# First node products from a turned x inside the sort and bucket stages; six basis pieces and the edge factors inside node stage two

## The reference

```
# every layer: x = layernorm(x + layer(x))
# layer 0: relu(concat(x[src], x[dst]) @ W0.T + b0) summed at src    # = relu(P[src] + Q[dst]), P = x @ W0a.T + b0, Q = x @ W0b.T
# layer 1: h = x @ W1.T, 8 heads; score * (1 + et_emb[type8]) * weight, softmax over dst; sum of h[src]; + x; layernorm
# layer 2: x @ Wself.T + mean of neighbours @ Wneigh.T + bias; layernorm
# layer 3, twice: w[r] = sum over 30 bases of att[r, b] * basis[b]; gated messages by type of 2; + x @ root + bias
```

## Time and profile before

| | |
|---|---|
| runs, us | 1919.64, 1920.72, 1919.0 |
| the profiled execution, us | 1921.72 |
| its span, us | 1919.7 |
| TensorE busy | 1587.8 us, 83% |
| VectorE busy | 1174.5 us, 61% |
| GpSimd busy | 720.3 us, 38% |
| ScalarE busy | 472.1 us, 25% |
| DMA | 249.14 MB, mean 130 GB/s |

### The profile page before, as it was taken

One profiled execution on the slowest core, in us unless ns is written; L12 is line 12 of the kernel. 1 busy time (PEld: TensorE's weight loads), 2 busy tenths in 40 slices (PEclk: granted clock), 3 DMA queues, 4 the chain that ended last, 5 costly groups with the idle time before them and its releaser, 6 DMA issues. The chain is left out here.

```text
span 1919.7 us, 26410 instructions
## 1 busy us (share of the span) xinstructions
PE 1587.8 (83%) x7213; PEld 962.6 (50%) x7214; DVE 1174.5 (61%) x2310; ACT 472.1 (25%) x884; POOL 720.3 (38%) x605
## 2 busy tenths in 40 slices
PE   6854886786498999998777369997598899999998
PEld 5750653335444555554544335554246545864486
DVE  5768889993375777775577876664865732122222
ACT  3301113433112555554344210000110111001100
POOL 0008777865094776660000447775330010000000
PEclk9996898998698999999898679999799999999999
DMA  0007764006703766682387337776105202430033
GB/s 25 0 18 263 257 210 121 2 2 214 269 27 104 208 197 187 186 169 43 132 348 303 118 109 211 210 210 152 28 1 157 84 1 92 150 110 1 0 137 136
DMA packets 76357, 249.14 MB, mean 130 GB/s; under 512 B 14901, under 2 KB 28582, under 8 KB 68346
## 3 DMA queue, kind: packets, MB, share of 16 engines
q1 hardware_dynamic: 38618, 147.08, 21.3%
q0 software_dynamic: 34592, 96.87, 19.0%
q10 hardware_dynamic: 3072, 4.20, 0.8%
HBM read 215.93 MB, written 32.00 MB: 129 GB/s over the span
## 5 line engine op out<-in xcount | busy, mean ns | idle before, releaser
L669 POOL DMA_INDIRECT tab_slots<-slot_words,slot_address x160 | 253.1, 1582 | 224.8 <-issue 215.0
L698 POOL DMA_INDIRECT e_rows<-tab_h,idx_h x176 | 178.6, 1015 | 286.3 <-POOLq L50 213.1
L1453 PE MATMUL dense_pY<-weights,dense_xT_block 128*128 128x512 f32 x640 | 283.8, 600 | 0.0
L1501 PE MATMUL dense_pY<-parts,dense_number 128*128 128x512 f32 x1000 | 237.6, 399 | 6.6 <-DMA dense_number<-tab_edges_to 6.6
L1004 POOL DMA_INDIRECT e_rows<-tab_q,idx_q x192 | 182.4, 950 | 98.9 <-issue 39.2
L1501 PEld LDWEIGHTS dense_pY<-parts,dense_number 128*128 128x128 f32 x1000 | 188.4, 189 | 54.4 <-DMA dense_number<-tab_edges_to 8.1
L792 PE MATMUL e_pS<-e_rows,e_onehot_ring 128*128 128x512 f32 x352 | 193.7, 641 | 22.2 <-DVE e_rows L768 18.6
L1453 PEld LDWEIGHTS dense_pY<-weights,dense_xT_block 128*128 128x128 f32 x640 | 121.5, 193 | 143.1 <-issue 142.6
L1077 PE MATMUL e_pS<-e_rows,e_onehot_f 128*128 128x512 f32 x384 | 180.8, 594 | 0.0
L889 PE MATMUL count_pA<-count_onehot_d,count_onehot_s 128*128 128x512 f16 (+1 forms) x576 | 119.3, 351 | 41.4 <-DVE count_onehot_d L860 29.4
L768 DVE TENSOR_TENSOR e_rows<-e_rows,e_pW 128x1024 f32<-128x1024 f32 x88 | 107.3, 1219 | 68.9 <-DMA e_rows<-tab_h,idx_h 68.8
(11 more groups left out here) (312 smaller groups left out, 2402.4 us busy)
## 6 DMA issues: line engine op xcount, KB each, us to landing
basis_piece<-in_L_gnn_basis_pieces SPq DMA_DIRECT2D x32, 2048.0 KB, 8.7
dense_number<-tab_edges_from SPq DMA_DIRECT2D x20, 1280.0 KB, 5.4
tab_edges_from<-counts_turned SPq DMA_DIRECT2D x10, 1280.0 KB
tab_edges_to<-counts_total SPq DMA_DIRECT2D x10, 640.0 KB
dense_number<-tab_edges_to SPq DMA_DIRECT2D x10, 640.0 KB, 4.5
tab_w<-basis_wout ACTq DMA_DIRECT2D x128, 32.0 KB
weights<-tab_w SPq DMA_DIRECT2D x4, 1024.0 KB, 6.5
weights<-in_L_gnn_W_T SPq DMA_DIRECT2D x3, 1024.0 KB
```

The costliest lines, as they stand in the source:

```text
L669: pool.indirect_dma_start(self.table, bass.IndirectOffsetOnAxis(self.address[:, t:t + 1], 0), self.words[:, t, :], None).then_inc(self.pla ...
L698: pool.indirect_dma_start(self.rows[:, q, s, :], None, self.table, bass.IndirectOffsetOnAxis(self.idx[:, j * 2 + s:j * 2 + s + 1], 0)).the ...
L1453: ins = self.nc.tensor.matmul(self.banks.at(g), self.xt[:, b % 2, c, :], weights[:, c, :], start=c == 0, stop=c == 3)
L1501: ins = self.nc.tensor.matmul(self.banks.at(self.first + b), self.number[:, b % 2, r * NB + k, :], self.parts[r][n][:, k, :], start=k == 0 ...
```

## The change

The diff does six things.

- A new class `FirstNodes` makes the 20 products of x with W0a and W0b (n = 2b + w for block b and weight w) from an x that arrives turned, so without transposes. The host lays out x.T as one more input. Its loads are issued by SP in the first load stage, after the constants.
- Four of the 20 products are written into the second part of the sort, product 0 ahead of the first small product, 1 to 3 ahead of the gather. ScalarE copies P to `acc` and Q to a ring of two, and SP stores Q.
- The other 16 are in the bucket stage, four ahead of the pair of products in its middle. The six basis pieces leave this stage.
- The placed columns are 32, 42, 56 and 30 in the four stages, before 24, 48, 68 and 20.
- Node stage one is gone. Load stage two adds the bias on GpSimd, copies the high part on ScalarE and subtracts on VectorE, ahead of VectorE's clearing of `acc`. x itself is loaded there, and the space in which it lies served the turned x, the one-hots of counting and the turned counts before.
- Node stage two takes the six basis pieces, one behind each of the blocks 0 to 5 on TensorE, with the copies and stores on ScalarE and the loads on SP, and the edge factors on GpSimd. Its loops on TensorE, ScalarE and SP are written out.

```diff
+class FirstNodes:
+    def load(self, sp, x_T, weights):
+        sp.dma_start(self.x_T[:, :, 0:N], x_T.rearrange("(c p) n -> p c n", p=P)).then_inc(self.loaded, 16)
+        for tile, source in zip(self.weights, weights):
+            sp.dma_start(tile, source).then_inc(self.loaded, 16)
+    def multiply(self, pe, n):
+        b, w = n // 2, n % 2
+        if n == 0:
+            pe.wait_ge(self.loaded, 48)
+        wait(pe, self.moved, n - 3)
+        for c in range(4):
+            ins = self.nc.tensor.matmul(self.py[:, n % 4, :], self.x_T[:, c, b * P:(b + 1) * P],
+                                        self.weights[w][:, c, :], start=c == 0, stop=c == 3)
+        ins.then_inc(self.multiplied, 1)
+    def move(self, act, n):
+        b, w = n // 2, n % 2
+        act.wait_ge(self.multiplied, n + 1)
+        if w == 0:
+            self.nc.scalar.copy(self.p[:, b, :], self.py[:, n % 4, :]).then_inc(self.moved, 1)
+        else:
+            wait(act, self.stored[b % 2], b // 2 * 16)
+            self.nc.scalar.copy(self.y[:, b % 2, :], self.py[:, n % 4, :]).then_inc(self.moved, 1)
+    def store(self, sp, b):
+        sp.wait_ge(self.moved, b * 2 + 2)
+        sp.dma_start(self.table[b * P:(b + 1) * P, :], self.y[:, b % 2, :]).then_inc(self.stored[b % 2], 16)
...
 # sort_edges, second part, TensorE
+                nodes.multiply(pe, 0)
                 pe.wait_ge(tot_ready, 1)
...
                                  ).then_inc(summed, 1)
+                for n in range(1, FIRST_NODES_IN_SORT):
+                    nodes.multiply(pe, n)
                 pe.wait_ge(prefix_ready, 1)
...
 # bucket_edges, TensorE
-            mix(0, 4)
+            for n in range(FIRST_NODES_IN_SORT, FIRST_NODES_IN_SORT + 4):
+                nodes.multiply(pe, n)
             pe.wait_ge(counted, 1)
...
-            mix(4, basis.steps * 4)
+            for n in range(FIRST_NODES_IN_SORT + 4, 2 * NB):
+                nodes.multiply(pe, n)
...
-PLACED_WITH_BUCKETS, PLACED_WHILE_PLACING, PLACED_WHILE_COUNTING = 24, 72, 140
+PLACED_WITH_BUCKETS, PLACED_WHILE_PLACING, PLACED_WHILE_COUNTING = 32, 74, 130
...
 # node_stage
+        def mixed_after(b):
+            return range(b * 2, b * 2 + 2) if 0 <= b < basis.steps * 2 else range(0)
...
+            for b in range(NB):
+                turn(b, b % 2)
+                if b:
+                    multiply(b - 1, (b - 1) % 2)
+                for n in mixed_after(b):
+                    basis.multiply(pe, n // 4, n // 2 % 2, n % 2)
...
+            for b in range(NB):
+                normal.roots(act, b)
+                if b >= 2:
+                    finish(b - 2, b % 2, b // 2 - 1)
+                copy_x(b, b % 2)
+                for n in mixed_after(b - 1):
+                    basis.store(act, n // 4, n // 2 % 2, n % 2)
...
+            basis.load_some(sp, 0, 2)
+            for b in range(NB):
+                if b < basis.steps * 2 - 2:
+                    basis.load_some(sp, b + 2, b + 3)
+                sp.wait_ge(act_out, b + 1)
...
 # gnn, load stage two
+                sp.dma_start(vec[:, 0, :], ins[VECS[0]].partition_broadcast(P)).then_inc(bias_in, 16)
                 table.read_back(sp, flat(slots[:, :, :]), slots_read)
...
+                for b in range(NB):
+                    act.wait_ge(biased, b + 1)
+                    nc.scalar.copy(p_parts[0][:, b, :], acc[:, b, :]).then_inc(high_out, 1)
                 act.wait_ge(score_w_out, 1)
...
+            def _(pool):
+                pool.wait_ge(bias_in, 16)
+                for b in range(NB):
+                    nc.gpsimd.tensor_tensor(acc[:, b, :], acc[:, b, :], V["L0_gnn_b"], ALU.add).then_inc(biased, 1)
...
+                nc.vector.memset(X[:, NB - 1, :], 0.0).then_inc(x_zero, 1)
+                for b in range(NB):
+                    v.wait_ge(high_out, b + 1)
+                    nc.vector.tensor_tensor(p_parts[1][:, b, :], acc[:, b, :], p_parts[0][:, b, :].bitcast(F32),
+                                            ALU.subtract).then_inc(low_out, 1)
+                v.wait_ge(low_out, NB)
                 link(nc.vector.memset(acc[:, :, :], 0.0))
...
-            node_stage(nc, "n0", X, C.f("ident"), take_x, 0,
...
-                   narrow=(score_w, (est, edt)))
+                   narrow=(score_w, (est, edt)),
+                   beside=EdgeFactor(nc, "factor", ins["L1_gnn_et_emb"], types[:, :], weight, factor), basis=basis[0])
```

More of the change, by code:

```diff
@@ L200, in load, with load_some @@
         peeled(eng, self.steps, step)
+    def load_some(self, eng, first, last):
+        if first == 0:
+            eng.dma_start(self.mix[:, :], self.mix_in).then_inc(self.mixed, 16)
+        for n in range(first, last):
+            wait(eng, self.used, (n - 1) * 2)
+            eng.dma_start(self.piece[:, n % 2, :], self.pieces[(n + self.first) * P:(n + self.first + 1) * P, :]
+                          ).then_inc(self.loaded[n % 2], 16)
     def start_multiply(self, pe):
@@ L2159, in _ @@
                     sp.dma_start(C.t[:, :], consts).then_inc(const_in, 16)
+                    nodes.load(sp, ins["x_T"], [turned_rows(ins, "L0_gnn_W", rows) for rows in (0, D)])
                     sp.wait_ge(zero_ready, 1)
@@ L2373 @@
         laid[name] = _np.asarray(inputs[name])
+    laid["x_T"] = _np.asarray(inputs["x"]).T
     for name in _TURNED:
```

137 lines of the change are left out of this document (70 added, 67 removed).

## The result

The changed kernel takes 1888.9 us, the median of four runs (1885.3 to 1893.5), beside 1919.3 (1917.4 to 1920.7) for the kernel before in the same session: a ratio of 0.985, 95% interval 0.983 to 0.988. The forecast was 1886.0, its range 1867 to 1905. The profiled execution took 1886.7, span 1884.9.

The account below looks back on a forecast made before the run. Each stage ends in a barrier, so only the engine that ends it last counts. Terms +14.8 (sort, bucket), -1 (placing, counting, storing), -69.2 (load, node stage one) and +22 (node stage two) sum to -33.4: 1886 us, range 1867 to 1905.

Parts of the forecast that it names:

- +14.8 for +14.8: Sort +3 and bucket stage +12: GpSimd's eight more placements at 1.48 us end the bucket stage, so both together +14.8 us.
- The price of a product, 3.5 us: Sort and bucket stage: a product of x and one weight, four f32 matmuls, takes TensorE 3.5 us.
- -3.9 for -1: Placing and counting: fewer placements give nothing in placing (bound -3) and -1 us in counting (at most -3.2).
- nothing, +3 as bound: Stage of stored counts: thirty placements for twenty end at 495.4, before the next stage at 506.39, so no cost; bound +3.
- -66.7 for -69.2: Load stage and removed node stage one: a bias, subtraction, clearing and unpacking chain of 28.2 us replaces 97.4, so -69.2 us.
- +23.2 for +22: Node stage two: pieces at TensorE's pace +14, including +4 waiting for piece 0, plus +8 from slower blocks; bounds +10 and +38.
- the +8: Node stage two: late ScalarE roots and GpSimd's factors stretch blocks from 6.9 to some 8.5 us, for about five blocks.
- near 78 us: Sign of being right: node stage two's length, with turned blocks 2 to 6 being 8 to 9 us apart.
- (B): Rival, 0.27: node stage two stays at TensorE's pace, +14, and the bias chain is at its short end: 1875 us.
- (C): Rival, 0.15: GpSimd and VectorE exclude each other in every SBUF operation, slowing node stage two and load chain: 1906 us.
- (D): Rival, 0.04: TensorE's clock stays at 1.2 GHz in the bucket stage's products, 7 us each instead of 3.5: 1947 us.
- records of a product at double length: Sign of being wrong: TensorE's product records last twice as long, as with the 1.2 GHz clock.

Follow-up runs that it names:

- experiment 1: Changed kernel with GpSimd's placements shared out as 28, 42, 78 and 12 in place of 32, 42, 56 and 30: 1879.5 us.
- experiment 2: Changed kernel with one first product in the sort and nineteen in the bucket stage, in place of four and sixteen: 1885.5 us.
- Experiment 8: Changed kernel with load stage two's slot words unpacked first and the accumulator cleared block by block behind the subtractions: 1887.7 us.
- experiment 7: Changed kernel with node stage two's basis pieces one block later on TensorE, ScalarE and SyncE: 1879.8 us, the stage 76.5 for 82.1.
- experiment 6: Changed kernel with ScalarE's copies and stores of a piece put behind the next block's root: 1886.8 us, node stage two 83.2 us.
- experiment 3: Changed kernel without node stage two's edge factors, set to one by a single instruction: 1883.0 us, the stage 73.0 us.
- experiment 5: Changed kernel with each of GpSimd's fifteen long factor instructions split in four: 1893.4 us, node stage two 80.7 us.
- experiments 4: Changed kernel without node stage two's six basis pieces, a 1 MB copy from the input in their place: 1888.1 us, the stage 77.8 us.
- five together: Changed kernel with placements 28, 45, 79, 8, pieces one block later, blockwise clearing, edge embedding loaded earlier, factor instructions halved: 1867.7 us, in a later session 1862.0.

## Why the prediction was right, point by point

**Direction and size.** Right: 1888.9 for 1886.0, a gain of 30.4 us for 33.4 in the terms. The -5.7 us behind node stage two that bring the profiled execution below the sum are no part of the change: in the same kernel's second profile the edge-score stage takes 133.7 us, all behind node stage two 978.4 (before, 977.9), and the medians are 1888.9 and 1889.9. Without them the terms add to -29.1. That the profiled execution, with -34.8, came so close to the sum is luck: three terms came out 1.2 to 3.4 us worse, placing and counting 2.9 better, and the draw gave 5.7.

**Sort and bucket stage.** Right, +14.8 for +14.8 and by the mechanism given: GpSimd's eight more placements, 1.49 us each. The price of a product, 3.5 us, was too low for the first eight (6.1, three of 4.1 and four of 4.2); product 0 fitted under the scan all the same, VectorE's first take of the gather came 2.7 us later than before (113.61 against 110.92) and the stage ended 2.3 us later, and in the bucket stage TensorE started 1.6 us before the forecast's 143.8 and had 5 us to spare. Experiments 1 and 2 bracket it: with 28 placements the two engines end together, with 19 products TensorE ends the stage.

**Placing and counting.** -3.9 for -1, inside the bounds, but not by the mechanism given. Counted between VectorE's first instructions, placing took 93.4 to 94.5 us in six profiles with 42 or 45 placements (before, 96.2 with 48) and counting 153.1 and 153.3 with 56, 153.0 to 153.5 with 78 or 79 (before, 154.9 with 68): fewer placements don't show as a gain, more not as a cost. Of counting's 1.6 us 0.95 lie ahead of its first one-hot (3.40 to 2.45 us), where a clearing of x is gone. The rest, and placing's 2 us, stay open.

**Storing.** Wrong: "nothing, +3 as bound", measured +3.4. The step that failed looked only at when the last placement ends, and it does end 14 us before the stage. But the placements slow the stores beside them. Thirty placements gave 64.3 us, twenty (in the kernel before) 60.9, twelve 57.6 and 57.8, eight 54.7 and 54.8: some 0.4 us each over the whole, 0.7 between twelve and eight. The forecast could have read this from the stores' spacing in SyncE's timeline of the kernel before, where the last placement ends at 478.4:

```profile
482.38 0.32 SPq L966 DMA_DIRECT2D tab_edges_to<-counts_total  x1
...
488.48 0.32 SPq L966 DMA_DIRECT2D tab_edges_to<-counts_total  x1
...
493.07 0.32 SPq L966 DMA_DIRECT2D tab_edges_to<-counts_total  x1
...
497.66 0.32 SPq L966 DMA_DIRECT2D tab_edges_to<-counts_total  x1
```

The spacing falls from 6.1 us to 4.6, some 10 us after that end.

**Load stage.** -66.7 for -69.2; the chain was the one described and 30.7 us long, between its bounds of 24 and 35. Three of its terms were short: the bias landed after 3.5 us for 3, the ten additions took 15.85 for 15, and the last copy and subtraction, with their waits, 2.5 for 1.5. (Node stage one was 82.1 us long, from 521.73 to 603.80, not 77; the sum does not use it.) Experiment 8 shows what an addition's pitch of 1.59 us (1.67 from the third on) is made of: 1.24 us with no subtraction beside it, and the rest a hold by VectorE's subtraction. The hold is mutual: a subtraction takes 1.53 us beside the additions and 0.63 behind them.

**Node stage two.** +23.2 for +22, but the parts behind the sum were not those. The wait for piece 0 was +4 in the forecast and is 6.0 in the trace, 5.6 of them on the path (experiment 7). The pieces at TensorE's pace, wait included, were right in sum: 14.1 us with the pieces alone, for +14. The step that failed is the +8 from "two copies and four issued stores" ahead of the root, together with the normalization: taking the late root away gave nothing (experiment 6), and turned blocks are 7.40 us apart, not 8 to 9. What makes a block 7.40 us is GpSimd's cycle for one type, to which VectorE's block is tied because its scale can end only when the long instruction ends. The factors cost 9.0 us on top of the pieces and would cost 18.9 without them. So the +8 was nearly the right size for half of the reason, and the total within 1.2 us is partly luck. (The forecast's sign "near 78 us" does not follow from its own term: 58.9 + 22 is 80.9.)

**The rivals.** (B) asked for TensorE's pace in node stage two; experiment 3 shows that pace, 6.67 us a block, where the factors are gone, and experiment 5 where their instructions are short; in the changed kernel it does not come. (C) had its mechanism right for the scale and the sum, though not for every operation from SBUF (see the last section), and its price wrong. The forecast held 767 ns for the subtraction beside 2702 for the scale against it. This was a misreading: the subtraction always followed a scale that had just been let go, so it fell into GpSimd's short instructions. GpSimd and VectorE, timelines of node stage one in the kernel before:

```profile
541.62 3.22 POOL L1358 TENSOR_TENSOR edge_factor<-edge_factor,factor_part 128x1408 f32<-128x1408 f32 x1
544.93 0.70 POOL L1351 TENSOR_SCALAR factor_of_type<-types 128x176 f32<-128x176 f32 x1
...
541.86 3.27 DVE L1220 TENSOR_SCALAR p_high<-n_upper_bits 128x512 fp32r<-128x512 f32 x1
545.05 0.81 DVE L1221 TENSOR_TENSOR p_low<-n_tmp,n_upper_bits 128x512 fp32r<-128x512 f32 x1
```

In experiments 4 and 6, where a two-input operation (the sum) meets the long instruction, it takes 3.65 us. The same timeline shows the types there 7.50 us apart (537.43 to 544.93), so the pitch of node stage two could have been read from it too. The rule of the Trainium skill (SBUF — State Buffer, on the port pair that GpSimd and VectorE share) holds in these runs: an operation with two inputs from SBUF is excluded for the whole of a GpSimd instruction that reads SBUF, as the sum, 3.65 us for 0.69, is until 0.5 us after GpSimd's addition. In the changed kernel it cost less than (C) said since there the late root puts the scale into GpSimd's long addition and the sum behind it, into short instructions (0.81 us); the two holds don't fall into the same block. (D) did not come: twelve products took 3.45 us each in the bucket stage (41.45 / 12) and the first four 4.2. Its sign, records of a product at double length, did show in product 0 of the sort: up to 1.19 us, where most take 0.59.

## What to carry to other kernels

When work is moved beside other work, ask not only when it ends but what it does to the pace of its neighbour: placements beside stores cost 0.4 us each though the last of them ended 14 us before the stage, and GpSimd's long instructions set the pitch of a stage in which TensorE was counted as the bound. A mean duration of an operation beside another engine's work says nothing of a hold unless the timelines show that the two met. Two loads put on one stage should each be taken away alone: 14 and 19 us made 23, and taking one away gives back only what the other doesn't cover. A sum that comes out right is no proof of its terms: here two of them were right in size for a wrong or unproven reason.

## What the runs showed that was not expected

- Which of VectorE's instructions are held. Beside GpSimd's tensor instructions the scale of 128x512, the sum of two SBUF tiles and the 0.25 us integer steps of the unpacking end with GpSimd's. A clearing (0.48 us) and the batch statistics don't: in five together the statistics take their usual 0.69 us inside a GpSimd instruction that runs from 819.61 to 821.34 and is itself the longer one (1.73 against 1.40 us), since VectorE's sum still ran when it began.

```profile
817.92 2.16 DVE L2382 TENSOR_TENSOR acc<-acc,x 128x512 f32<-128x512 f32 x1
820.23 0.69 DVE L1187 BATCH_NORM_STATS2 n_bn<-acc 128x6 f32<-128x512 f32 x1
...
819.61 1.73 POOL L1424 TENSOR_TENSOR factor_part<-factor_of_type,factor_emb 128x704 f32<-128x704 f32 x1
```

- TensorE's granted clock in the sort. The profile gives 1.00 throughout from 92 to 140 us in the kernel before. With the four products it gives 1.00 up to 100, 0.86 up to 112 and 0.60 from there to 140. In experiment 1 it stays at 1.00 up to 112 (0.53 from there), and the same three products take 10.50 us instead of 12.19, about as much as that sort gains. This is no chance of one execution: all four profiles with 28 placements show 10.50 us and 1.00, all eight others with four products 12.1 to 12.2 us and 0.86, though the placements come only after the sort. Nor is it the amount of work: with product 0 alone (experiment 2) the clock is 0.61 from 100 to 112 and 0.50 behind it. Product 0 itself has records of double length in a stretch marked 1.00. The cause is not shown, and neither is that the edit of the placements is what does it.
